# Layer 1 of a recommendation tower: two parts and a longer end, other orders, ids first, W1 in pieces

## The reference

```
e  = stack of 40 table rows per sample       # 512 samples x 40 fields x 32
z[b,k] = e[b,i] @ W[k] @ e[b,j]              # the 780 pairs k = (i, j), i < j
h  = concat(z, dense_ctx)                    # 780 + 16 values
h  = relu(h @ W_top1 + b_top1)               # 796 x 512
h  = relu(h @ W_top2 + b_top2)               # 512 x 256
y  = h @ W_top3                              # 256 x 1
```

## Time and profile before

| | |
|---|---|
| median of three runs (lowest to highest) | 190.03 us (189.29 to 190.49) |
| profiled execution: its time, its span | 191.81 us, 190.0 us |
| mean granted clock of PE in it | 0.991 of full speed |
| busy in the span: PE, DVE, ACT, POOL | 174.8, 148.2, 92.0, 115.8 us |
| DMA engines' mean busy share over the slices | 90% or more from 66.5 to 71.3 us (W1 and W2 are issued at 64.6), under 20% from 76 us on |

### The profile page before, as it was taken

The page is one execution under the profiler, slowest core; times in us unless marked ns, Lnnn a source line. Parts: engine busy times, 40 slices in busy tenths (PEclk is TensorE's granted clock), DMA queues, the critical chain, the costliest instruction groups (busy, mean ns, idle before and its releaser), DMA issues.

```text
span 190.0 us, 4602 instructions
## 1 busy us (share of the span) xinstructions
PE 174.8 (92%) x1976; PEld 47.3 (25%) x1976; DVE 148.2 (78%) x141; ACT 92.0 (48%) x83; POOL 115.8 (61%) x107
## 2 busy tenths in 40 slices
PE   1999949998999996999999999999999799999993
PEld 0243303321233222122122112222222122222331
DVE  0999987999999786598899898897975868882500
ACT  4877995989699520261072335252255332230421
POOL 0777777877877777778777777877068180522000
PEclk9999999999999999699999999999999999999999
DMA  5999310100000194000111000000000000000000
GB/s 187 388 410 337 106 17 10 19 10 17 16 14 16 39 352 147 17 10 10 17 14 17 11 14 16 13 14 14 3 3 0 0 3 3 0 0 3 0 3 0
DMA packets 7164, 10.80 MB, mean 57 GB/s; under 512 B 2004, under 2 KB 4696, under 8 KB 7144
## 3 DMA queue, kind: packets, MB, share of 16 engines
q1 hardware_dynamic: 3896, 8.81, 12.6%
q0 software_dynamic: 3072, 1.58, 4.8%
q10 hardware_dynamic: 176, 0.12, 0.3%
HBM read 10.50 MB, written 0.00 MB: 55 GB/s over the span
## 4 chain that ended last, share of the span: by engine, by line
PE 55%; POOL 26%; issue 8%; DMA 6%; DVE 2%; ACT 2%; ACTq 0%; DVEq 0%
POOL rows L375 26%; PE ring_ps L595 21%; PE z_ps L612 16%; PE ring_ps L621 13%; PE ring_ps L659 4%; DMA rows<-table,idx 4%; DMA idx<-ids 2%; DVE prod L314 2%; ACT copied L423 1%; PE ring_ps L580 1%; ACT h L458 0%; ACT emb L412 0%; PE ring_ps L665 0%; ACTq L436 0%; DVE y_sb L521 0%
## 5 line engine op out<-in xcount | busy, mean ns | idle before, releaser
L375 POOL DMA_INDIRECT rows<-table,idx x96 | 99.0, 1031 | 33.7 <-issue 28.9
L314 DVE TENSOR_TENSOR prod<-ring_ps,emb 128x1024 f32<-128x1024 f32 x73 | 86.8, 1220 | 16.4 <-PE ring_ps L595 15.6
L595 PE MATMUL ring_ps<-emb,wall 32*64 32x512 f32 (+1 forms) x800 | 61.2, 620 | 3.6 <-DVE prod L314 2.3
L423 ACT ACTIVATE copied<-ring_ps 128x1024 f32<-128x1024 f32 x27 | 27.6, 1025 | 57.7 <-PE ring_ps L595 54.8
L612 PE MATMUL z_ps<-prod,consts_sb 128*32 128x512 f32 x400 | 50.7, 609 | 0.1
L314 DVE TENSOR_TENSOR prod<-copied,emb 128x1024 f32<-128x1024 f32 x20 | 26.6, 1333 | 5.0 <-ACT copied L423 5.0
L314 POOL TENSOR_TENSOR prod<-copied,emb 128x1024 f32<-128x1024 f32 x7 | 16.6, 2377 | 22.5 <-ACT copied L423 22.5
L621 PE MATMUL ring_ps<-zt,w_sb 128*32 128x512 f32 x224 | 26.7, 597 | 0.0
L595 PEld LDWEIGHTS ring_ps<-emb,wall 32*64 32x64 f32 (+1 forms) x800 | 12.9, 131 | 44.3 <-issue 21.1
L399 ACT ACTIVATE distance<-ids,vocab 128x2048 f16<-128x2048 f16 x10 | 20.0, 2000 | 1.7 <-PE ring_ps L567 1.2
L402 ACT ACTIVATE one_hot<-distance,vocab 128x2048 bf16<-128x2048 f16 x10 | 20.0, 2002 | 0.3
(11 more groups left out here) (25 smaller groups left out, 56.4 us busy)
## 6 DMA issues: line engine op xcount, KB each, us to landing
w_sb<-w SPq DMA_DIRECT2D x1, 1792.0 KB, 8.0
rows<-table,idx POOLq DMA_INDIRECT x96, 2.4
table<-hot_table SPq DMA_DIRECT2D x2, 640.0 KB, 5.5
table<-hot_table SPq DMA_DIRECT2D x2, 512.0 KB, 4.1
wall<-w_pairs SPq DMA_DIRECT2D x1, 640.0 KB
wall<-w_pairs SPq DMA_DIRECT2D x1, 576.0 KB, 9.1
wall<-w_pairs SPq DMA_DIRECT2D x1, 512.0 KB, 8.1
w_sb<-w SPq DMA_DIRECT2D x1, 512.0 KB, 9.8
```

Source lines behind the costliest of these rows:

```text
L314: return eng.tensor_tensor(prod[:, o % RING_P], products, emb[:, slots:slots + 1, :].to_broadcast([P, 2, BATCH]), ALU.mult)
L375: nc.gpsimd.indirect_dma_start(rows[:, k, c, r, :], None, tables[f], bass.IndirectOffsetOnAxis(ap=idx[:, c, f:f + 1], axis=0)).then_inc(ga ...
L423: nc.scalar.activation(copied_op(o), op_banks(o), ACT.Copy).then_inc(copied_ready, 1)
L595: mm = nc.tensor.matmul(pair(("map", g), i // 2)[half, i % 2, :], wall[own, g, half], emb[own, stream, :], start=True, stop=True)
```

## The change

Layer 1 has two parts of two z tiles each, in place of three parts (two, two and one tile), and the end takes three z tiles in place of two; so its first stretch has two tiles for each block. All orders, the banks, the lists of operations that POOL multiplies and that are copied, and the one-hots that ACT makes are other ones. The ids of the gather are SP's first DMA and no longer ACT's second. W1 is loaded in three pieces, one for each part and one for the end, each with a semaphore of its own, and its issue waits also for the landing of the third gathered quad; W2 has its own semaphore.

```diff
@@ -91,28 +91,29 @@
 RING_TABLE = 3
 RING_HOT = 2
 RING_COPY = 4
-PARTS = [(0, 1), (2, 3), (4,)]
-TAIL = (5, 6)
-TENSOR_ORDER = ("iillllllilllilllllmllmmtlllmlsllslmlllmmssmsmmstslmlllmlslmlllmmlsmssmssmstmsmsmm1mssmssm1mstmmsmssm"
-                "1msmsm1mstmsmmssmssm1mssm1mssm1mtmmssmssm1mssmssms1m11msssmm1s")
-BANKS = ("0240624304042065202024024024660240240240240206420242064024026403042402460242026406204024020640241422"
-         "4642604204246024024604320402462301")
-VECTOR_ORDER = ("rooooorooooooooooroowwwwooowworwwwwwwwwwooowwwowowwwwwwwwwwwwwwwwwwwwwwwwwwwwwwwwwwwwwwwwwwwwwwwwwww"
-                "wwwawwwwaawwwwwawwwwwwwaawawwwa")
-SCALAR_ORDER = ("IIoIIIIILIoLoLooLooLooozLcccLzc1cLcc1zc1c1ccLcczcccccLcccczcccczc")
-POOL_OPS = [77, 78, 80, 85, 87, 93, 98]
-COPIED_OPS = [28, 32, 34, 37, 45, 47, 48, 54, 56, 60, 62, 64, 67, 69, 73, 75, 81, 84, 89, 92]
-SCALAR_ONE_HOTS = [4, 17, 21, 23, 25, 27, 30, 31, 34, 35]
+W1_BEHIND = 2
+PARTS = [(0, 1), (2, 3)]
+TAIL = (4, 5, 6)
+TENSOR_ORDER = ("iiilllllilllllllllllmmmtslmlllmllmllllsmssmssmmtslmllsmlllmlllmmlsmssmstmsmssmmsm1mssmssm1mtsmsmmssm"
+                "1mssm1mssmtsmmsmssm1m1m1msmstmssmsmmsmsmsmsm1mssmssmssmsms")
+BANKS = ("0240246025024066240240240240662402402402402642024020462402406246024204260420642046204024062460462040"
+         "624024204204204062402402406452")
+VECTOR_ORDER = ("roooooooroooooooorwoowwwoowowowwwrwwwwowwwowowowowwwwwwwwwwwwwwwwwwwwwwwwwwwwwwwwwwwwwwwwwwwwwwwwaww"
+                "awwwwawwwwwwwwwwawwwwwwww")
+SCALAR_ORDER = ("IIIIIIoILIoLoLooLooLooozLcLcczc11cLz11cLzcccccccLcccccczcccccccccz")
+POOL_OPS = [73, 75, 76, 79, 85, 88, 93, 96, 98]
+COPIED_OPS = [28, 30, 34, 37, 47, 62, 69, 70, 74, 80, 81, 82, 83, 84, 89, 90, 91, 92, 95]
+SCALAR_ONE_HOTS = [6, 16, 20, 22, 25, 27, 29, 30, 34, 35]
 def z_place(t):
@@ -235,7 +236,8 @@
         vocab_loaded = sem("vocab_loaded")
         const_loaded = sem("const_loaded")
         ctx_loaded = sem("ctx_loaded")
-        mlp_loaded = sem("mlp_loaded")
+        w1_loaded = [sem(f"w1_loaded{part}") for part in range(len(PARTS) + 1)]
+        w2_loaded = sem("w2_loaded")
         wload = [sem(f"wload{q}") for q in range(QUADS)]
         gathered = [sem(f"gathered{k}") for k in range(len(GATHERED_AT))]
         hot_ids_loaded = sem("hot_ids_loaded")
@@ -346,6 +348,7 @@
                 sp.dma_start(wall[:, first:first + q + 1, :].rearrange("p g n -> p (g n)"),
                              w_pairs[:, first * P:(first + q + 1) * P]).then_inc(wload[q], 16)
+            sp.dma_start(idx[:].rearrange("p c f -> p (c f)"), ids).then_inc(ids_loaded, 16)
             load_table(0)
             sp.dma_start(vocab[:], vocab_rows).then_inc(vocab_loaded, 16)
             load_table(1)
@@ -360,8 +363,11 @@
                 load_table(h)
             sp.dma_start(ctx_sb[:], ctx_rows).then_inc(ctx_loaded, 16)
             sp.wait_ge(one_hot_used, FIRST_ONE_HOT[-1])
-            sp.dma_start(w1_sb[:], w1.rearrange("k p n -> p k n")).then_inc(mlp_loaded, 16)
-            sp.dma_start(w2_sb[:], w2.rearrange("(k p) n -> p k n", p=P)).then_inc(mlp_loaded, 16)
+            sp.wait_ge(gathered[W1_BEHIND], 16 * SLOTS * CHUNKS)
+            for part, ks in enumerate([*PARTS, TAIL]):
+                own = slice(ks[0], ks[-1] + 1)
+                sp.dma_start(w1_sb[:, own, :], w1[own].rearrange("k p n -> p k n")).then_inc(w1_loaded[part], 16)
+            sp.dma_start(w2_sb[:], w2.rearrange("(k p) n -> p k n", p=P)).then_inc(w2_loaded, 16)
             sp.wait_ge(y_saved, 1)
             sp.dma_start(out.rearrange("(c b) o -> c (b o)", b=P), y_sb[::DIM, :]).then_inc(stored, 16)
             sp.wait_ge(stored, 16)
@@ -434,7 +440,6 @@
                                      bias=b1_sb[:, m:m + 1]).then_inc(lin_saved, 1)
             act.dma_start(ids_sb[:], hot_ids).then_inc(hot_ids_loaded, 16)
-            act.dma_start(idx[:].rearrange("p c f -> p (c f)"), ids).then_inc(ids_loaded, 16)
             act.wait_ge(hot_ids_loaded, 16)
             nc.scalar.activation(ids_rows[:], ids_sb[:], ACT.Copy).then_inc(ids_rows_done, 1)
             for kind, what in ACT_STEPS:
@@ -636,24 +641,27 @@
                 else:
                     part, m = what
                     pe.wait_ge(z_saved, PARTS[part][-1] + 1)
-                    pe.wait_ge(mlp_loaded, 32)
+                    pe.wait_ge(w1_loaded[part], 16)
                     banks_free(("layer1", what))
                     layer1(bank(("layer1", what)), PARTS[part], m).then_inc(lin_done, 1)
-            pe.wait_ge(z_saved, TAIL[0] + 1)
+            pe.wait_ge(z_saved, TAIL[-2] + 1)
+            pe.wait_ge(w1_loaded[len(PARTS)], 16)
             for m in range(M1):
                 banks_free(("tail", m))
-                layer1(bank(("tail", m)), TAIL[:1], m, stop=False)
+                layer1(bank(("tail", m)), TAIL[:-1], m, stop=False)
                 if m == 0:
                     sum_ops(LAST // 2)
             pe.wait_ge(lin_saved, len(PARTS) * M1)
             pe.wait_ge(last_z_saved, 1)
             for m in range(M1):
-                layer1(bank(("tail", m)), TAIL[1:], m, start=False).then_inc(lin_done, 1)
+                layer1(bank(("tail", m)), TAIL[-1:], m, start=False).then_inc(lin_done, 1)
             for m in range(M2):
                 for k in range(M1):
                     if m == 0:
                         pe.wait_ge(h1_ready, k + 1)
+                    if m == 0 and k == 0:
+                        pe.wait_ge(w2_loaded, 16)
                     for c in range(COLUMNS):
                         first = m * P + DIM * c
                         mm = nc.tensor.matmul(h2_ps[m][DIM * c:DIM * (c + 1), :], w2_sb[:, k, first:first + DIM],
```

## The result

The changed kernel took 188.2 us (median of 20 runs, 187.49 to 190.2), the kernel before 189.94 beside it: a ratio of 0.992, 95% interval 0.990 to 0.994. The forecast was 187.5 within 185.6 to 190.2. The gain is 1.7 us, under the 1% that I had called faster; the likeliest case, 1.3% faster, did not come, and the next one, within 1%, did.

A forecast was written before the change was run, and what follows sets the result against it. PE was taken to be paced by POOL's gathers up to the last turn: 134.3 + 32.9 + 8.6 + 10.5 = 186.3, with 1.2 of waits a span of 187.5, 2.5 below 190.0; taken from the median: 187.5, range 185.6 to 190.2.

The forecast's parts named there:

- the likeliest case: Whole kernel: faster than 188.1 us, beyond the 1% a measurement can tell; chance 0.52.
- the next one: Whole kernel: time within 1% (1.9 us) of the kernel before; chance 0.40.
- Ids first: Head of the gathers: ids issued 0.44 us earlier on SP's queue, landing unchanged; ends nothing and 1.4.
- W1 behind the third gather: Load of W1 after the third quad: costs nothing, at most 0.8 us; third quad lands 2.53 after its gather.
- The orders: PE's six turns: each reached at or before its gather, last turn at 134.3, 6.1 us before 140.40.
- counts of letters: PE's work between turns, from step prices: 20.3, 20.5, 21.2, 20.1 and 20.3 us.
- signs of being wrong: In the trace after: last turn behind its gather, stretch behind it over 34.5 us, or first gather not earlier.
- Behind the last turn: Last turn to end of last sum: 32.9 us of PE work, 1.2 of waits (ends 0 and 1.75).
- My walk: New order stepped through with its banks: each bank freed in time to 0.2 us, latencies left out.
- The rival that the median lacks the slow stretch: Clock on PE: 1.5 us of gain absent from the median, or paid after new waits; 189.0, chance 0.36.
- the slower rival: POOL's gathers held up 4.2 us by W1's pieces: 191.7; chance 0.09 with other ways to be slower.
- That the change does not do what it says: Third quad lands as late as before, W1 not being what held it: 189.8 us; chance 0.05.

The follow-up runs named there:

- kernel without late gathers: Changed kernel with POOL gathering two quads only, later turns rereading the second quad's rows, W1 waiting for the second quad: 188.13 us, ratio 0.9928.
- second profile of before: The kernel before, unchanged, run and profiled again: 190.02 us, span 188.2, granted clock 1.000.
- the ids first and the parts: Kernel before with ids first, two parts and a three-tile end, the one-tile steps and their additions taken out, old order otherwise: 191.43 us, ratio 1.0055.
- W1 early: Changed kernel without W1's wait for the third gathered quad: six runs, 190.33 and 190.52, and 194.23 to 195.23, beside 190.25 for the kernel before.

## Why the prediction held its range and missed its case

*Ids first: the term that was mis-sized.* I took the 0.44 of earlier issue. The first gather came 1.85 earlier (5.18 to 3.33): the issue gave 0.44 and the landing shrank from 3.72 to 2.32, which is beyond the far end of 1.4 that I had drawn from the hot ids' 2.8. The page of the Trainium skill that I had weighed against it (DMA: Bandwidth & Descriptors, Issuing engines are not separate DMA queues) would have given 0.44, and the measurement decides: on this kernel the move to the head of another queue also made the landing 1.4 shorter. That the ids had followed the hot ids on ACT's queue may be the reason. The hot ids point to it: issued at 0.73 before and 0.74 after, they release ACT 0.66 earlier without the ids behind them. Timeline of ACT, before and after:

```profile
3.57 0.64 ACT L439 ACTIVATE ids_rows<-ids_sb 16x528 f16<-16x528 int32 x1 [0.63 <-DMA ids_sb<-hot_ids]
...
2.91 0.64 ACT L444 ACTIVATE ids_rows<-ids_sb 16x528 f16<-16x528 int32 x1 [0.45 <-DMA ids_sb<-hot_ids]
```

Another reason is as possible: before, the first table's load was issued ahead of the ids, at 0.74 on SP's queue, and now behind them. The two were not tried apart.

*W1 behind the third gather.* The mechanism was right for the new order, which loses the whole gain and more without it, and wrong for the old one: with the ids first, the old order meets no wait there at all. Costing the wait at nothing was right.

*The orders: the step that failed.* I wrote that PE would reach each turn at or before its gather and be paced by POOL to the last turn. With 1.4 more of earlier gathers, and a pace that was quicker by 2.6 over the stream (95 steps in 124.4, before 127.0), PE came behind its gathers from the third turn on. What sets POOL's pace no run shows. The counts of letters held: from the second to the last turn they give 20.5 + 21.2 + 20.1 + 20.3 = 82.1, the trace 83.3. The 2.2 us by which the last turn was earlier than forecast come from the second turn (48.74 for 49.45) and from gathers that I had let PE wait for. The kernel without late gathers keeps its time, so from the second turn on it is not POOL that paces PE but PE's own work. Two of the three signs of being wrong that I had named came: the last turn behind its gather (132.06, the gather in at 130.25), and the stretch behind it over 34.5.

*Behind the last turn.* Counted 32.9 and 1.2 of waits; the window from 132.06 to the end of the last sum is 34.84, so the waits are 1.9, just over the end that I had kept. Most of it is one cycle, in four maps in a row, which stand 1.14 in all. Timeline of the changed kernel, PE and ACT:

```profile
140.98 1.12 PE L600 MATMUL ring_ps<-emb,wall 32*64 32x512 f32 x16 [0.27 <-ACT copied L429]
...
142.19 1.94 ACT L429 ACTIVATE copied<-ring_ps 128x1024 f32<-128x1024 f32 x2 [0.43 <-PE ring_ps L600]
143.36 1.12 PE L600 MATMUL ring_ps<-emb,wall 32*64 32x512 f32 x16 [0.26 <-ACT copied L429]
...
144.56 1.02 ACT L429 ACTIVATE copied<-ring_ps 128x1024 f32<-128x1024 f32 x1 [0.43 <-PE ring_ps L600]
...
145.73 1.12 PE L600 MATMUL ring_ps<-emb,wall 32*64 32x512 f32 x16 [0.26 <-ACT copied L429]
```

A map begins, ACT's copy of its first half begins 1.2 later, takes 1.02, and the next map's second half needs that bank: 2.37 from map to map, where PE has 2.04 of work. My walk had given the first half of a map out after half its time; the rows show both halves ready only with the whole map. Behind the last sum I had 19.1, and the trace has 186.0 - 166.9 = 19.1.

*The base and the clock.* The rival that the median lacks the slow stretch was right in its first half: the second profile of before has none. I had seen that the profiled execution was 1.8 above the median and subtracted the whole change from the median all the same, after charging the old trace with 1.5 of lost clock. The sum that I had made was a span, 187.5, which is a run of about 189.3. The measured span is 186.0: the last turn came 2.24 earlier than forecast, the stretch behind it took 0.74 more than 32.9 + 1.2, and the end was as counted. So the span was forecast 1.5 too long, and the step from the span to the time was left out, 1.8 too short. The size came out near because two errors met: that is luck, not a right mechanism. The Trainium skill (TensorE: Matmul & The Clock Gate, Part 1) says that idling brings the slow clock back. The profile with the ids first and the parts agrees, with half clock after 1.74 of wait; the changed kernel hardly waits, and its profile has a mean clock of 1.000.

*The sides.* Gathers slowed by W1's pieces, the slower rival, did not come: the 16 gathers from the 48th on took 21.6 (65.38 to 87.02), where before they took 21.7. That the change does not do what it says was refuted for the ids.

## What to carry to other kernels

When one engine issues a long serial stream (here 96 gathers), look first at what the stream itself waits for: one DMA moved to the head of another queue gave all that the whole change did. Before a profile is used as the base of a sum, compare its run's time with the range of the runs; if it lies outside, its extra waits and slow clock are not yours to win. And after a change of many edits, run each alone: the orders here needed the loading edits to be harmless, and the loading edits did not need the orders.

## What the runs showed of the hardware

Four matmuls of 512 columns took 1.88 us at 6.43 and 1.03 at 14.74 in the same kernel, while the granted clock reads 1.00 over the earlier stretch: ahead of the first change of clock the duration of a known step is the safer witness. And the length of a wait did not decide alone what came after it: half clock followed 1.74 us of wait with the ids first and the parts and 1.79 in the first profile of before, full clock followed 2.12 at its first turn and 1.68 with W1 early (mean clock of that execution 1.000).
